# k of a linear attention made token-major by its own products, with the bias opening the banks

## What is computed

```
q = gelu(x @ Wq + bq) + 0.21
k = gelu(x @ Wk + bk) + 0.21
v = x @ Wv + bv
q_r, k_r = rope(q), rope(k)
kmean = mean(k, over tokens)
z = 1 / (q . kmean + 1e-06)
kv = k_r^T v / n                 # per head
x = layernorm((q_r kv) * z + x)
```

## Time and profile before

| | |
|---|---|
| median of three runs | 1950.24 us |
| the profiled execution | 1948.09 us, its span 1946.3 us |
| TensorE busy | 1914.7 us, 98% |
| VectorE, ScalarE, GpSimd busy | 69%, 51%, 55% |
| attention | from about 186 to 1088 us |
| granted clock of TensorE | 0.99 over the span, 0.50 from 171.9 to 184.4 us |

### The profile page before, as it was taken

One profiled execution on the slowest core, in us unless ns is written; L12 is line 12 of the kernel. 1 busy time (PEld: TensorE's weight loads), 2 busy tenths in 40 slices (PEclk: granted clock), 3 DMA queues, 4 the chain that ended last, 5 costly groups with the idle time before them and its releaser, 6 DMA issues.

```text
span 1946.3 us, 47536 instructions
## 1 busy us (share of the span) xinstructions
PE 1914.7 (98%) x19756; PEld 1573.1 (81%) x19756; DVE 1344.0 (69%) x3296; ACT 983.8 (51%) x1803; POOL 1063.2 (55%) x973
## 2 busy tenths in 40 slices
PE   8998999999999999999999999999999999999998
PEld 2335888888888888888888799999999999999997
DVE  3555566766676667667766865968686867777776
ACT  4443566766676676667666663232323222322231
POOL 1453898998898889888988401221212131312221
PEclk9997999999999999999999999999999999999999
DMA  7343310122000301121011672101010101010100
GB/s 274 128 164 147 129 35 34 34 77 77 34 2 34 121 34 34 34 72 49 14 35 56 199 234 93 43 33 34 33 44 22 44 23 44 22 44 22 44 11 22
DMA packets 26247, 128.04 MB, mean 66 GB/s; under 512 B 4592, under 2 KB 5168, under 8 KB 19888
## 3 DMA queue, kind: packets, MB, share of 16 engines
q1 hardware_dynamic: 20240, 87.20, 12.6%
q0 software_dynamic: 2304, 25.17, 3.8%
q10 hardware_dynamic: 3488, 12.64, 1.7%
HBM read 93.53 MB, written 31.46 MB: 64 GB/s over the span
## 4 chain that ended last, share of the span: by engine, by line
PE 85%; POOL 2%; issue 1%; DMA 1%; DVE 0%; ACT 0%; POOLq 0%; DVEq 0%; SPq 0%
PE bankC L34 12%; PE bankC L32 12%; PE bankC L33 12%; PE ring L32 6%; PE ring L34 6%; PE ring L33 6%; PE big L885 4%; PE big L32 3%; PE big L34 3%; PE big L33 3%; PE ring L816 3%; PE big L796 3%; PE big L892 3%; PE ring L860 2%; PE ring L838 2%; PE acc L32 2%
## 5 line engine op out<-in xcount | busy, mean ns | idle before, releaser
L32 PE MATMUL bankC<-down_hi,act_hi 128*128 128x256 f32 x1024 | 288.7, 282 | 0.0
L34 PE MATMUL bankC<-down_hi,act_lo 128*128 128x256 f32 x1024 | 286.3, 280 | 0.0
L33 PE MATMUL bankC<-down_lo,act_hi 128*128 128x256 f32 x1024 | 285.9, 279 | 0.0
L1491 DVE TENSOR_TENSOR act_lo<-gel,act_hi 128x512 fp32r<-128x512 f32 x256 | 210.6, 823 | 8.8
L1453 POOL TENSOR_TENSOR rstdC<-var_epsC,minus_halfC 128x4 f32<-128x4 f32 x48 | 53.6, 1116 | 277.1 <-DVE var_epsC L1516 277.1
L1447 POOL TENSOR_TENSOR hC<-hC,vecC 128x1024 f32<-128x1024 f32 x16 | 38.8, 2424 | 303.5 <-PE turn L1364 303.5
L34 PE MATMUL bankC<-aT_hi,up_lo 128*128 128x512 f32 x512 | 202.4, 395 | 0.0
L33 PE MATMUL bankC<-aT_lo,up_hi 128*128 128x512 f32 x512 | 202.2, 395 | 0.0
L32 PE MATMUL bankC<-aT_hi,up_hi 128*128 128x512 f32 x512 | 202.1, 395 | 0.0
L33 PEld LDWEIGHTS bankC<-down_lo,act_hi 128*128 128x128 f32 x1024 | 192.2, 188 | 1.6
L32 PEld LDWEIGHTS bankC<-down_hi,act_hi 128*128 128x128 f32 x1024 | 192.1, 188 | 1.5
(11 more groups left out here) (195 smaller groups left out, 5391.3 us busy)
## 6 DMA issues: line engine op xcount, KB each, us to landing
w_first<-w_split POOLq DMA_DIRECT2D x8, 1536.0 KB, 7.2
w_second<-w_split POOLq DMA_DIRECT2D x8, 1536.0 KB, 8.9
raw_late<-in_AB SPq DMA_DIRECT2D x30, 320.0 KB, 4.1
xs<-in_x_conv SPq DMA_DIRECT2D x16, 513.0 KB, 7.2
u<-hA SPq DMA_DIRECT2D x8, 1024.0 KB, 4.2
u_next<-u SPq DMA_DIRECT2D x8, 1024.0 KB, 5.5
hC<-u SPq DMA_DIRECT2D x16, 512.0 KB, 3.9
xC<-in_x SPq DMA_DIRECT2D x16, 512.0 KB, 4.9
```

The lines of the kernel that those rows point to most:

```text
L32: e.matmul(out, wh, xh, start=start, stop=False)
L33: e.matmul(out, wh, xl, start=False, stop=False)
L34: return e.matmul(out, wl, xh, start=False, stop=stop)
L1491: e.tensor_tensor(a_lo[:, fb, :], g, a_hi[:, fb, :].bitcast(F32), ALU.subtract).then_inc(s_act_lo, 1)
```

## The change

k's product is made with the two operands' roles exchanged: the tokens are loaded in the array, 128 at a time, and the 256 columns of k's weights are streamed. The result is tokens by channels at once, so turn_k and gkT go. A bias per channel lies along the columns then and can't be ScalarE's per-partition bias. It comes in by one more product per bank: 32 rows of a constant 1/16 (16 rows with the high part of the bias, 16 with the low part) by bias_k, over all 512 columns of the bank. ScalarE applies Gelu in place in the bank. VectorE adds the two tokens tiles of each bank in a reduction (k_two), then the four of those (k_four, k_all); TensorE sums over the partitions by a one-column product per 128 channels, between values 0 and values 1; ScalarE adds 0.21 T and spreads the mean, behind the copy of v. The ring has ten places a unit in place of 14. kr moves to the place of gkT.

In Prep the one-column products of k go, and products of the shift by k's weights, 256 columns in 32-column shapes, come first; VectorE forms bias_k from them; k's given bias is loaded on all partitions; the weights' loads of layers 1 to 3 share a semaphore. The diff, cut to its core:

```
-        TURN = ([("k", b) for b in range(4)] + [("kt", u) for u in range(4)] + [("q", 0), ("q", 1)] +
-                [("q", 2), ("q", 3), ("den", 0), ("kv", 0)])
+        TURN = [("k", u) for u in range(4)] + [("q", b) for b in range(4)] + [("den", 0), ("kv", 0)]
...
+            def project_k(n, u):
+                wt = weights(n, H, H)
+                bank = ring_of(n, "k", u)
+                rows = slice(D * u, D * u + D)
...
+                w.wait_ge(s_lo, 4 * n + 2 * (u // 2) + 2)
+                e.matmul(bank[:, :], sixteenth[rows, :], bias_k[rows, layer(n), :].unsqueeze(1).broadcast_to([D, 2, H]),
+                         start=True, stop=False)
+                for t in range(2):
+                    tok = slice((2 * u + t) * P, (2 * u + t + 1) * P)
+                    for cb in range(CB):
+                        m = mm3(e, bank[:, t * H:(t + 1) * H], (hT_hi[:, cb, tok], hT_lo[:, cb, tok]), wt[cb], False,
+                                t == 1 and cb == CB - 1)
+                m.then_inc(s_k, 1)
...
-            def turn_k(n, u):
-                bank = ring_of(n, "kt", u)
-                w.wait_ge(s_gk, 4 * n + 2 * (u // 2) + 2)
-                w.wait_ge(*ring_empty(n, "kt", u))
-                for t in range(2):
-                    for db in range(CB):
-                        m = e.transpose(bank[:, t * H + db * P:t * H + (db + 1) * P],
-                                        gkT[:, db, (2 * u + t) * P:(2 * u + t + 1) * P], identity[:, :])
-                m.then_inc(s_kt, 1)
+            def sum_k(n):
+                bank = ring_of(n, "den", 0)
+                w.wait_ge(*ring_empty(n, "den", 0))
+                w.wait_ge(s_ksum, 2 * n + 2)
+                for db in range(CB):
+                    m = e.matmul(bank[:, 2 * P + db:2 * P + db + 1], k_all[:, db * P:(db + 1) * P], ones[:, :], start=True, stop=True)
+                m.then_inc(s_kall, 1)
...
-                project(n, 1, "k", 0)
-                project(n, 1, "k", 1)
-                turn_k(n, 0)
-                turn_k(n, 1)
+                project_k(n, 2)
+                project_k(n, 3)
                 if n >= 1:
                     outputs(n - 1)
-                turn_k(n, 2)
-                turn_k(n, 3)
-                project(n, 0, "q", 0)
-                project(n, 0, "q", 1)
+                project_q(n, 0, 0)
+                project_q(n, 0, 1)
...
+            def gelu_k(n, u):
+                bank = ring_of(n, "k", u)
+                w.wait_ge(s_k, 4 * n + u + 1)
+                e.activation(bank[:, :], bank[:, :], ACT.Gelu).then_inc(s_gk, 1)
             def k_mean(n):
-                w.wait_ge(s_ksum, n + 1)
+                w.wait_ge(s_memset, 1)
+                w.wait_ge(s_kall, n + 1)
                 w.wait_ge(s_den, n)
                 w.wait_ge(d_consts, 3 * 16)
+                e.activation(km[:, :], ring_of(n, "den", 0)[:, 2 * P:2 * P + CB], ACT.Identity,
+                             bias=sum_shift[:, 0:1]).then_inc(s_km, 1)
+                w.wait_ge(s_km, 2 * n + 1)
...
                 e.scalar_tensor_tensor(pairs(kr[:, u, :]), pairs(bank[:, :])[:, :, ::-1], 0.21, pairs(table(sin_k)),
-                                       ALU.add, ALU.mult).then_inc(s_ks, 1)
+                                       ALU.add, ALU.mult)
+                e.tensor_reduce(k_two[:, u, :], bank[:, :].rearrange("p (t n) -> p n t", t=2), X, ALU.add).then_inc(s_ks, 1)
...
+            def sum_k(n):
+                w.wait_ge(s_ks, 4 * n + 4)
+                e.tensor_tensor(k_four[:, :, :], k_two[:, 0:2, :], k_two[:, 2:4, :], ALU.add).then_inc(s_ksum, 1)
+                w.wait_ge(s_ksum, 2 * n + 1)
+                w.wait_ge(s_kall, n)
+                e.tensor_tensor(k_all[:, :], k_four[:, 0, :], k_four[:, 1, :], ALU.add).then_inc(s_ksum, 1)
```

In Prep.tensor and vector_biases:

```
+        for l in range(L):
+            e.wait_ge(*self.landed(l))
+            for cb in range(CB):
+                for i in range(4):
+                    m = e.matmul(self.rows_ps[l // 2][32 * i:32 * i + 32, l % 2 * H:(l % 2 + 1) * H], self.shift[:, l * CB + cb, :],
+                                 self.raw[:, l, cb, H:2 * H], start=cb == 0, stop=cb == CB - 1)
+        m.then_inc(self.s_rows, 1)
...
+        e.wait_ge(self.s_rows, 1)
+        for i in range(2):
+            two = self.k_in[:, 2 * i:2 * i + 2, :].rearrange("p l n -> p (l n)")
+            e.tensor_tensor(two, self.rows_ps[i][:, :], two, ALU.add).then_inc(v, 1)
+        e.wait_ge(v, 3)
+        e.tensor_copy(self.k_hi[:, :, :], self.k_in[:, :, :]).then_inc(v, 1)
+        e.wait_ge(v, 4)
+        e.tensor_scalar(self.bias_k[:, :, :], self.k_hi[:, :, :].bitcast(F32), self.sign[:, 0:1], None, ALU.mult).then_inc(v, 1)
+        e.wait_ge(v, 5)
+        e.scalar_tensor_tensor(self.bias_k[:, :, :], self.k_in[:, :, :], parity[:, 1:2], self.bias_k[:, :, :].bitcast(F32),
+                               ALU.mult, ALU.add)
         e.wait_ge(self.s_bias, 1)
```

More of the change, by code:

```diff
@@ L466, in allocate @@
         self.shift = sb("shift_col", [P, L * CB, 32])
-        self.qk_in, self.v_in = sb("bqk_in", [P, 4 * L]), sb("bv_in", [P, L, 2 * 32])
+        self.q_in, self.k_in, self.v_in = sb("bq_in", [P, CB * L]), sb("bk_in", [P, L, self.H]), sb("bv_in", [P, L, 2 * 32])
+        self.k_hi, self.sign = sb("bk_hi", [P, L, self.H], F32R), sb("sign", [P, 1])
         self.block = sb("head_block", [P, 2 * 32])
-        self.d_raw = [sem(f"d_raw{l}") for l in range(L)]
+        first, others = sem("d_raw_first"), sem("d_raw")
+        self.d_raw = [first] + [others] * (L - 1)
+        self.landed = lambda l: (self.d_raw[l], 16 * (L - 1) if l else 16)
         self.d_in, self.d_out = sem("d_in"), sem("d_out")
-        self.s_hi, self.s_lo, self.s_bias, self.s_v = sem("hi"), sem("lo"), sem("bias"), sem("v")
+        self.s_hi, self.s_lo, self.s_rows, self.s_bias, self.s_v = sem("hi"), sem("lo"), sem("rows"), sem("bias"), sem("v")
     def due(self, n, after):
@@ L589, in attention_phase @@
         cos_k, sin_k, cos_q, sin_q = (place[n] for n in ("cos_k", "sin_k", "cos_q", "sin_q"))
-        hT_hi, hT_lo, gkT, kc = (place[n] for n in ("hT_hi", "hT_lo", "gkT", "kc"))
+        hT_hi, hT_lo, kr, kc = (place[n] for n in ("hT_hi", "hT_lo", "kr", "kc"))
         identity = keep["identity"]
@@ L967, in gelu_q @@
                 for db in range(CB):
-                    at = layer(n) * 2 * CB + db
+                    at = layer(n) * CB + db
                     bank = ring_of(n, "q", 2 * x + db)
                     w.wait_ge(s_q, 4 * n + 2 * x + db + 1)
-                    e.activation(bank[:, :], bank[:, :], ACT.Gelu, bias=bias_qk[:, at:at + 1]).then_inc(s_gelu, 1)
+                    e.activation(bank[:, :], bank[:, :], ACT.Gelu, bias=bias_q[:, at:at + 1]).then_inc(s_gelu, 1)
                     w.wait_ge(s_gelu, 4 * n + 2 * x + db + 1)
@@ L1006, in scalar @@
                 split_u(n, 1)
-                gelu_k(n, 0)
-                gelu_k(n, 1)
+                for u in range(DUOS):
+                    gelu_k(n, u)
                 if n >= 1:
                     copy_out(n - 1)
-                k_mean(n)
                 gelu_q(n, 0)
@@ L1156, in vector @@
                     copy_turned(n - 1)
-                rotate_k(n, 0)
-                k_mean(n)
-                for u in range(1, DUOS):
+                for u in range(DUOS):
                     rotate_k(n, u)
+                sum_k(n)
                 if n >= 1:
@@ L1734, in take @@
                                     ALU.subtract).then_inc(s_out_lo, 1)
-            wait_free(w, before.free["gkT, kc"])
+            wait_free(w, before.free["kr, kc"])
             for n in range(len(duos)):
@@ L1815, in build @@
         attention = attention_phase(nc, t["u0"], t["u4"], T, H, t["w_split"],
-                                    {n: t[n] for n in ("cos_k", "sin_k", "cos_q", "sin_q")}, t, bias_qk, bias_v, keep, place,
+                                    {n: t[n] for n in ("cos_k", "sin_k", "cos_q", "sin_q")}, t, bias_q, bias_k, bias_v, keep, place,
                                     ctx, d_u0, d_u4, prefetch)
```

129 lines of the change are left out of this document (63 added, 66 removed).

## The result

| | kernel before | changed kernel |
|---|---|---|
| median of the runs | 1950.87 us | 1978.94 us (1978.13 to 1981.28) |
| profiled execution | 1948.09 us, span 1946.3 | 1981.28 us, span 1979.5 |
| ratio of the runs | 1 | 1.0146, 95% interval 1.0128 to 1.0163 |
| one unit of attention, mean of 31 | 28.05 us | 28.83 us |
| first turning of u to first key_value | 31.13 us | 33.69 us |

The changed kernel is slower by 28.1 us. The two profiled executions are 33.2 us apart, and that sum closes: 31 x 0.78 = 24.2 us in the units, 2.6 in the first unit, 3.8 ahead of attention, 2.7 behind it (the rest, from the start of the last key_value to the end of the span, takes 862.7 us against 860.0; in all the kernels with GpSimd's order unchanged it lies between those two, in no order that I can read).

The account below looks back on a forecast made before the run. TensorE's own queue was taken as the bound: -1.69 + 0.06 + 1.95 + 0.44 = +0.76 us a unit, +24.3 us over 32 units, nothing before attention, giving 1974 us on the 1950.24 median; range 1950 to 1986.

Parts of the forecast that it names:

- The turnings: TensorE's queue in each attention unit: 16 turnings of k leave, 0.86 and 0.83 us, together -1.69 us.
- the k products: TensorE in each unit: 24 products of 512 columns become 48 of 256, 5.60 to 5.65 us, +0.06 us.
- the one-column products: TensorE between values 0 and values 1: the sum over tokens adds four records of 0.109 us, +0.44 us a unit.
- The bias products: TensorE: four 32-row products opening k's banks, with shape changes and unhidden loads, +1.95 us a unit, bounds 0.70 and 2.5.
- the case without hand-overs: Lower bound for the four bias products if 32 rows stand among full-array products like any other: 0.70 us a unit.
- Rival (a): TensorE's 32-row products cause no drain: bias costs 0.70, a unit changes by -0.49 us, total 1934.5 us; chance 0.12.
- GpSimd's chain is unchanged: GpSimd in each unit: same chain, starting 0.4 us later in a longer unit.
- VectorE's small sums: VectorE after the four bank reductions: two small sums over tokens, about 1.0 us of the +3.5 us a unit.
- the sign that I gave: VectorE would still be idle before attention's turned outputs if the forecast was right.
- the cover of 1.19 us: VectorE's wait for the turned outputs after its last rotation, from 709.26 to 710.45, expected to keep added work from delaying anything.
- Rival (c): k's mean late on ScalarE, or VectorE's reductions delay q's banks: 0.3 to 0.5 us a unit, 1984 to 1990; chance 0.14.
- Before attention: Preparation of biases, k's bias load included: phase ends about where it does, 0 us, bounds -2 and +2.

Follow-up runs that it names:

- the fastest form: Changed kernel with 128-row bias products, k's bias loaded during the convolutions, GpSimd's first invert ahead of rotate_q, VectorE's token sums accumulated straight from the banks: 1937.57 us.
- the running sum: Changed kernel with 128-row bias products and k's bias loaded during the convolutions, VectorE adding each bank half straight into k_all, GpSimd's order old: 1947.93 us.
- The kernel before with its early invert: Kernel before the change, with only GpSimd's invert(n - 1, 0) moved ahead of rotate_q(n, 0, 0): 1962.44 us, ratio 1.0076.
- the late load: Changed kernel with the load of k's bias issued during the convolutions on its own semaphore, not at the start: 1976.64 us, ratio 1.0128.

## Why the prediction was right, and where it was off

Forecast 1974, range 1950 to 1986; measured 1978.94. The side, the mechanism and the unit were right; the start was not.

- **The turnings, -1.69; the k products, +0.06; the one-column products, +0.44.** Without the bias products the fastest form's unit is 26.89; these three terms give 28.05 - 1.69 + 0.06 + 0.44 = 26.86, from the mean unit of the kernel before (I had read one unit, of 28.12). Only their sum is shown, and the one-column products by themselves: 0.48.
- **The bias products, +1.95.** Measured 1.93. Also the end that I kept for the case without hand-overs, 0.70, was met: 0.65 with the full shape, three slots and none at k2. The way there was right too: 0.42, 0.62, 0.30 and 0.62 us at the four places against my 0.42, 0.63, 0.37 and 0.63. By the mean unit, 28.05 + 0.76, it was to be 28.81 and is 28.83. That it is so near is partly luck: I took 0.21 us as streaming, since two slots of 0.118 were 0.02 longer than one of 0.233, and they are 0.003 longer. The stream costs its whole slot of 0.23, and the two changes of shape with their loads 0.39 where I had 0.42; the two errors cancel. The Trainium skill, "TensorEngine Tiling (Array Packing)", Key Properties, has the rule that a change of tiling mode drains TensorE; these runs agree for 128*128 beside 32*128 and beside 64*128, at 0.39 us for the pair of changes with the loads that are no longer hidden; they don't part the one from the other.
- **Rival (a), 1934.5 if there is no drain, was priced wrong** although its unit, 27.56, is what TensorE does in such a kernel. Made so that no drain occurs, the changed kernel took 1969.73. I had written that GpSimd's chain is unchanged and starts 0.4 us later; its round is 28.57 us long there, 1 us more than rival (a)'s unit. The step that failed is that I checked for new waits only against the forecast's unit, not against the rival's shorter one.
- **VectorE's small sums, about 1.0.** Measured 3.0. They have two operands in buffers and run beside GpSimd's four additions, which go from 5.03 to 5.65 us. What showed it is the running sum, with one operand in the bank: 0.42 a pass, and GpSimd back at 5.02. The Trainium skill, "SBUF — State Buffer", Who interferes with whom, says that a VectorE instruction with two inputs from SBUF contends with a GpSimd instruction that reads it; these rows agree. I had not weighed it, and the sign that I gave, VectorE idle ahead of the turned outputs, is absent: rotations and sums end 17.2 us after the start of key_value (730.78 - 713.61), where they were to end within 0.3 us of the 15.0 of today, and the cover of 1.19 us was used up to the last.
- **Rival (c), the mean or the sums too late,** did not happen in a unit: the mean had 0.43 us to spare where I gave it 0.2, and q waited for no bank. It did happen once, in the first unit, where no outputs of an earlier unit stand between k and q: that unit is 2.6 us longer, and my sum counted 32 equal ones. What starts it is the sine table. k comes to VectorE earlier, as I had written (ScalarE is through with the first bank at 201.6, 12.2 us after the first turning, where the first turned bank came after 16.1), but the table lands at 205.0 and VectorE can't begin before. From 205.09 on VectorE has three passes a bank instead of two, q's four products wait for their banks one after another (0.6, 0.3, 0.3 and 0.3 us more than a slot), and the one-column products wait 0.6 for k_all. Begun at 202.0, VectorE would have been ahead of all of them by the same rows (an estimate). That table was held back in no run, nor issued earlier.
- **Before attention, 0 with bounds of 2.** The preparation takes 189.44 - 173.04 = 16.4 us from the last convolution's turning, as in every form of the changed kernel, against 185.68 - 168.29 = 17.4. The kernel before with its early invert does the old preparation in 15.8, at a granted clock of 0.61 over it and not 0.54; so between 1.0 shorter and 0.6 longer, inside the bounds. The load of k's bias, which I had put inside the same bounds, is not hidden: about 2 us by the late load. The 4.8 us between the last turnings of the one pair of profiles are more than that, and a part of them comes and goes without the load. I had looked at the earlier trace rows, the end of the stage, and at no row of its start, where that transfer stands beside the raw weights.

The 4.9 us between forecast and median are mainly these last two: 1.8 in the first unit (2.6 where the sum had 0.76) and about 2 in the start. The rest is 0.6 in the other units (0.78 each for 0.76) and 0.6 because the kernel before has a median of 1950.87 here and not 1950.24.

## What to carry to other kernels

Give a small matmul among full ones the full array shape if its operands allow it; a fourfold number of rows costs less than two changes of shape. When the bound engine gets shorter, ask which round is next and how far behind it is, for every rival's unit and not for the forecast's alone; here the second round took four fifths of what the first one would have given. When data arrive earlier, ask what else their reader waits for: a table that landed 1.7 us ahead of its first use became a wait. And keep additions with both operands in SBUF off VectorE while GpSimd works there: a pass of 256 elements with one operand in a bank took 0.42 us and left GpSimd alone.

## What the runs showed of the hardware that I had not expected

- A bias product of 64 rows among products of 128 costs as much as one of 32 rows (units of 28.86 and 28.83 us), one of 128 rows 0.39 us less where both neighbours have the full shape.
- VectorE's addition of 512 elements took 1.65 us and that of 256 elements 1.39 beside GpSimd's additions; an addition of 256 elements with one operand in PSUM 0.42. GpSimd's additions of 512 took 1446 ns with those beside them and 1286 without.
- A reduction of 512 elements in PSUM to 256 took 0.68 us, like any other pass of VectorE over 512.
- With a transfer of 512 KB issued at the start on ScalarE's queue beside the raw weights' loads, GpSimd's first work on them began 1.3 us later on the mean of the profiles (2.4 in the one pair).
- A block of 16 matmuls behind 4.15 us of idleness ran for 3.64 us and not 1.93, at a granted clock of 0.50; behind 3.03 us in another kernel the same; behind 3.40 us in the fastest form it ran for 1.93, at 1.00.
